# A gated cross-attention block with routed experts: normalisation of context and tokens moved from VectorE to ScalarE, and the gating slot reordered

## The reference

```python
x = x + tanh(g_xattn) * xattn(layernorm(x), ctx)   # 16 heads of 8, keys and values from the context
x = x + tanh(g_ffn) * ffn(layernorm(x))            # 8 experts, the best 2 of each token
```

## Time and profile before

| | |
|---|---|
| median of 3 runs | 401.38 us (397.15 to 403.08) |
| the profiled execution | 394.16 us, span 392.3 us |
| TensorE busy | 335.7 us (86% of the span) |
| VectorE busy | 236.9 us (60%) |
| ScalarE busy | 178.9 us (46%) |
| GpSimd busy | 105.5 us (27%) |

### The profile page before, as it was taken

How to read it: one execution, slowest core, us unless ns; L and a number is a source line. 1 busy time by engine, 2 the same in 40 slices (tenths; PEclk the granted TensorE clock), 3 DMA queues, 4 the chain that set the end, 5 groups by cost and what they waited for, 6 DMA issues and landing times.

```text
span 392.3 us, 8185 instructions
## 1 busy us (share of the span) xinstructions
PE 335.7 (86%) x2799; PEld 253.9 (65%) x2799; DVE 236.9 (60%) x935; ACT 178.9 (46%) x408; POOL 105.5 (27%) x188
## 2 busy tenths in 40 slices
PE   0869898789999789976999689979997998989693
PEld 0435565566787577855687477857785786677573
DVE  4693857665677456865477456866666566314553
ACT  1333445543745245543555246545654455334352
POOL 6473251434031603161031603150312001200000
PEclk9996989956999669976999869979998899558998
DMA  4411310363355431926055531815191500340000
GB/s 99 141 24 54 90 44 2 70 92 139 124 92 71 149 135 41 121 70 217 4 93 68 162 123 40 124 30 219 37 123 32 217 3 4 92 154 2 1 28 27
DMA packets 18456, 32.95 MB, mean 84 GB/s; under 512 B 4905, under 2 KB 11530, under 8 KB 18416
## 3 DMA queue, kind: packets, MB, share of 16 engines
q1 hardware_dynamic: 14270, 24.45, 24.9%
q0 software_dynamic: 3296, 7.93, 8.5%
q10 hardware_dynamic: 850, 0.05, 0.1%
HBM read 21.04 MB, written 2.21 MB: 59 GB/s over the span
## 4 chain that ended last, share of the span: by engine, by line
PE 36%; DVE 8%; DMA 6%; issue 3%; ACT 2%; POOL 1%; DVEq 0%; POOLq 0%
PE y L585 10%; PE c L532 5%; DMA gb<-gates_scratch 4%; PE s L510 3%; PE h L576 3%; PE ab L488 2%; PE h L577 2%; PE h L578 2%; DMA gates_scratch<-gatesT 2%; PE ab L549 2%; PE ab L556 1%; PE c L543 1%; PE ab L438 1%; DVE y_out L1073 1%; DVE negm L939 1%
## 5 line engine op out<-in xcount | busy, mean ns | idle before, releaser
L939 DVE TENSOR_REDUCE negm<-ab 128x4 f32<-128x308 f32 x128 | 59.5, 476 | 56.0 <-PE ab L488 55.0
L775 ACT ACTIVATE p<-s 77x512 f32<-77x512 f32 x128 | 74.9, 586 | 24.8 <-PE s L510 23.9
L510 PEld LDWEIGHTS s<-qs,ks 104*77 104x77 f32 x512 | 60.8, 168 | 11.0 <-issue 4.9
L585 PE MATMUL y<-w2s,hs 128*128 128x128 f32 x448 | 65.2, 292 | 1.3 <-ACT hs L782 1.3
L510 PE MATMUL s<-qs,ks 104*77 104x128 f32 x512 | 64.3, 254 | 0.1
L585 PEld LDWEIGHTS y<-w2s,hs 128*128 128x128 f32 x448 | 59.8, 207 | 1.8 <-ACT hs L782 1.7
L488 PE MATMUL ab<-ks,qs 96*128 96x312 f32 x128 | 55.0, 431 | 5.0 <-DVE negm L939 2.4
L532 PE MATMUL c<-p,vs 77*32 77x128 f32 x1024 | 54.5, 307 | 0.1
L782 ACT ACTIVATE hs<-u 128x512 f32<-128x512 f32 x56 | 35.1, 628 | 37.1 <-DVE u L1060 35.7
L1227 POOL TENSOR_SCALAR rs<-mv 128x1 f32<-128x1 f32 x32 | 8.0, 250 | 157.8 <-DVE mv L980 157.7
L1060 DVE SCALAR_TENSOR_TENSOR u<-h,gb 128x512 f32<-128x512 f32 x56 | 38.0, 681 | 17.9 <-DMA gb<-gates_scratch 16.0
(11 more groups left out here) (130 smaller groups left out, 525.8 us busy)
## 6 DMA issues: line engine op xcount, KB each, us to landing
gb<-gates_scratch SPq DMA_DIRECT2D x14, 768.0 KB, 5.7
gb<-gates_scratch SPq DMA_DIRECT2D x7, 512.0 KB, 3.8
qs<-q_hi SPq DMA_DIRECT2D x12, 256.0 KB, 5.5
ks<-k_hi SPq DMA_DIRECT2D x60, 39.0 KB
x_res<-in_x_dram POOLq DMA_DIRECT2D x8, 256.0 KB, 7.1
out_dram<-y_out POOLq DMA_DIRECT2D x8, 256.0 KB, 2.8
x_sb<-in_x_dram POOLq DMA_DIRECT2D x6, 256.0 KB, 3.7
qs<-q_lo SPq DMA_DIRECT2D x6, 256.0 KB, 7.7
```

Source lines behind the costliest of these rows:

```text
L510: mm = nc.tensor.matmul(p[0:N, T * i:T * i + T], ks[:, par, c, i, NP * j:NP * j + N], qs[:, par, c, T * j:T * j + T], start=True, stop=True)
L585: mm = nc.tensor.matmul(bank_y[:, D * b:D * b + D], hs[:, e % 2, T * b:T * b + T], w2s[:, e, :], start=(e == 0 and b == 0), stop=(e == E - ...
L775: nc.scalar.activation(p32[:, c, :], src, ACT.Exp).then_inc(p_done, 1)
L939: nc.vector.tensor_reduce(negm[:, :, c], bank_ab[bank][:, 0:J * NP].rearrange("t (i n) -> t i n", n=NP)[:, :, 0:N], AX.X, ALU.max, negate= ...
```

## The change

From tile 2 on, ScalarE computes context and tokens as scale * x + shift, with the root as scale and a shift = -mean * root, which GpSimd makes with two more instructions per chain (a negation of the mean and a product), so its chain has four instructions instead of two. Tiles 0 and 1 stay on VectorE; the eight instructions of each of tiles 2 to 7 leave it. On ScalarE the context stands behind exponent 1 of slot 2, the tokens behind exponent 2. In slot 1 VectorE starts the gates only behind `x_lo`, and takes its last two portions behind `mv`; the addition of `finish` moves behind the third portion. ScalarE does the first exponent of the next batch and the copy of the gates ahead of `evacuate_turned` in slot 1; in the other slots that order stays. TensorE and SyncE run the same instructions in the same order.

```diff
--- before.py
+++ after.py
@@ -51,7 +51,7 @@
 
 STATS = ["ctx_stats", "x_stats", "ctx_moments", "x_moments"]
 NORM = ["ctx_normed", "x_normed"]
-NORM_P = ["cvar_eps", "crstd", "var_eps", "rstd"]
+NORM_P = ["cvar_eps", "cneg", "crstd", "cshift", "var_eps", "neg", "rstd", "shift"]
 MAXP = ["hi", "lo"]
 POST = ["recip", "scaled", "x1", "stats", "moments", "normed"]
 LATE = ["top", "x_lo"]
@@ -133,7 +133,7 @@
         c_st = sb("c_st", [N, G, 6])
         x_mv = sb("x_mv", [T, G, 2])
         c_mv = sb("c_mv", [N, G, 2])
-        nrm = sb("nrm", [T, 4, G])
+        nrm = sb("nrm", [T, 6, G])
         xn = sb("xn", [T, G, D])
         cn = sb("cn", [N, G, L])
         xnT = sb("xnT", [D, GT])
@@ -729,6 +729,15 @@
                 nc.scalar.activation(q_hi[:, :], bank_ab[bank][:, :], ACT.Identity,
                                      bias=col(BQS)).then_inc(hi_q, 1)
 
+            def normalise(s, par, which):
+
+                n, dst, src, k, name = {"ctx": (N, cn, ctx_sb, 1, "cshift"), "x": (T, xn, x_sb, 4, "shift")}[which]
+                act.wait_ge(norm_p, at(NORM_P, s, name))
+                for b in range(G):
+                    ins = nc.scalar.activation(dst[:, b, :], src[:, par, b, :], ACT.Identity,
+                                               bias=nrm[0:n, k + 1, b:b + 1], scale=nrm[0:n, k, b:b + 1])
+                ins.then_inc(norm_d, 1)
+
             def split_query_rows(s, par):
 
                 if s == 0:
@@ -818,6 +827,8 @@
                         evacuate_heads(*near[-1])
                     if near[0]:
                         exponent(*near[0], 1)
+                    if j == 2 and third and i >= 0:
+                        normalise(*third, "ctx")
                     if j == 1 and exists(i - 1):
                         gate_exp(i - 1)
                     if j == 3 and third:
@@ -830,6 +841,8 @@
                         max_store(*near[2])
                     if near[0]:
                         exponent(*near[0], 2)
+                    if j == 2 and third and i >= 0:
+                        normalise(*third, "x")
                     if e[1] is not None:
                         squared(sf, e[1])
                     if j == 3 and third:
@@ -842,12 +855,14 @@
                         squared(sf, e[2])
                     if j == 2 and third:
                         evacuate_xT(third[0])
-                    if near[-1]:
-                        evacuate_turned(*near[-1])
-                    if near[1]:
+                    if j == 1 and near[1]:
                         exponent(*near[1], 0)
                     if j == 1 and spread(i - 1):
                         gate_rows(i - 1)
+                    if near[-1]:
+                        evacuate_turned(*near[-1])
+                    if j != 1 and near[1]:
+                        exponent(*near[1], 0)
 
             steps(step)
 
@@ -895,7 +910,7 @@
                 dve.wait_ge(norm_p, at(NORM_P, s, "rstd"))
                 for b in range(G):
                     ins = nc.vector.tensor_scalar(xn[:, b, :], x_sb[:, par, b, :], x_mv[:, b, 0:1],
-                                                  nrm[:, 3, b:b + 1], ALU.subtract, ALU.mult)
+                                                  nrm[:, 4, b:b + 1], ALU.subtract, ALU.mult)
                     if b == G - 1:
                         ins.then_inc(norm_d, 1)
                     if b % 2:
@@ -1139,7 +1154,7 @@
                     prepare = none
                     if j == 0 and third and i >= 0:
                         prepare = stats(*third)
-                    if j == 2 and third and i >= -1:
+                    if j == 2 and i == -1:
                         prepare = chained(normalise_ctx(*third), normalise_x(*third))
                     if j == 3 and third:
                         prepare = chained(low_keys(*third), (low_queries if i >= 0 else low_query_rows)(*third))
@@ -1160,26 +1175,21 @@
                         weighed(sf, pf, pending)
                     if near[-2]:
                         routed(*near[-2])
-                    take(gating)
                     take(top_scores)
                     take(post)
-                    take(gating)
                     take(top_scores)
-                    take(gating)
                     take(post)
-                    take(gating)
                     take(top_scores)
                     if near[-2]:
                         low_x(*near[-2])
                     take(gating)
                     take(gating)
-                    take(gating)
-                    if j == 1 and exists(i - 2) and not last(i - 2):
-                        finish(sf, pf)
                     take(top_scores)
                     if e[0] is not None:
                         gated_or_weighed(sf, pf, e[0])
                     take(gating)
+                    if j == 1 and exists(i - 2) and not last(i - 2):
+                        finish(sf, pf)
                     take(post)
                     take(top_scores)
                     take(post)
@@ -1213,12 +1223,16 @@
 
                 pool.wait_ge(stats_d, at(STATS, s, f"{which}_moments"))
                 apart(pool)
-                n, mv, k, scale, eps, names = {"ctx": (N, c_mv, 0, 1.0, EPS, ("cvar_eps", "crstd")),
-                                               "x": (T, x_mv, 2, 1.0 + EPS, EPS * EPS, ("var_eps", "rstd"))}[which]
+                n, mv, k, scale, eps, names = {"ctx": (N, c_mv, 0, 1.0, EPS, ("cneg", "crstd", "cshift")),
+                                               "x": (T, x_mv, 3, 1.0 + EPS, EPS * EPS, ("neg", "rstd", "shift"))}[which]
                 nc.gpsimd.tensor_scalar(nrm[0:n, k, :], mv[:, :, 1], scale, eps, ALU.mult, ALU.add).then_inc(norm_p, 1)
+                nc.gpsimd.tensor_scalar(nrm[0:n, k + 2, :], mv[:, :, 0], -1.0, None, ALU.mult).then_inc(norm_p, 1)
                 pool.wait_ge(norm_p, at(NORM_P, s, names[0]))
                 nc.gpsimd.tensor_tensor(nrm[0:n, k + 1, :], nrm[0:n, k, :], neg_half[0:n, :],
                                         ALU.pow).then_inc(norm_p, 1)
+                pool.wait_ge(norm_p, at(NORM_P, s, names[1]))
+                nc.gpsimd.tensor_tensor(nrm[0:n, k + 2, :], nrm[0:n, k + 2, :], nrm[0:n, k + 1, :],
+                                        ALU.mult).then_inc(norm_p, 1)
 
             def rstd(s, par, j):
                 n = G * s + j
```

## The result

The changed kernel has its median at 379.72 us over 4 runs (376.93 to 387.6); beside it the kernel before has 399.26 us (396.55 to 403.08). Intervals are computed from fast runs alone, those whose time is at most 1.5% above their kernel's fastest, while medians and ranges in the text are over all runs.

The account below looks back on a forecast made before the run. TensorE bounds the kernel, through its waits for VectorE's `cn` and the low clock behind them. Steps 2 to 4 give 13.8 us, the earlier L549 2.4, step 7 2: 18.2 us off 401.38, 383 us, range 368 to 396.

Parts of the forecast that it names:

- The copy of the gates: ScalarE, slot 1: copy ahead of the evacuation, store issues 2.4 us earlier in step 4, broadcast lands near 223.0.
- L414 waits for nothing, L585 waits 0.7 to 1 us, 8.1 us behind L549: TensorE, step 4: context transposes free, first output waits some 0.7 to 1 us for its square instead of 3.06.
- Steps 2, 3 and 4 give 13.8 us: These steps come down to step 5's length, 4.2 + 5.2 + 4.4 = 13.8 us, 6 of it clock.
- ScalarE's and GpSimd's prices: Normalising costs 1.5 us per four activations; GpSimd's negation 0.19 us and product 0.2 us.
- 0.4 us from the earlier L549 in steps 2 to 7: 2.4 us: VectorE's new gating order gives the moments earlier, moving the `xn2` transpose 0.4 us forward per step, 2.4 us together.
- rival 2: The low-clock stretch behind the L549 wait goes too, giving back 15 us: 368 us; chance 0.13.
- Step 7 2 us: Step 7's outputs lose a 1.1 us wait for a square behind the broadcast; 2 us with the clock.
- Step 0 has no gates to wait for: 0: Step 0, the first step, was counted as neither gaining nor losing.
- Normalising on ScalarE: Tiles 2 to 7: moving eight activations per tile off VectorE frees the context's transposes from the broadcast's landing.
- Rival 3: The waits go but the clock gives nothing back: gain 11 us, 390 us; chance 0.07.
- Rival 1: The stall moves on: gates' transfers land no earlier, L585 only 1.3 us earlier in five steps, 395 us; chance 0.19.
- Rival 4: Slower: negation and product at 1.04 us each make ScalarE late in every step, 412 us; chance 0.04.

Follow-up runs that it names:

- changed_again: The changed kernel with no edit, run once more in one set with orders_again: median 376.87 us.
- changed_third: The changed kernel with no edit, run again in the set of changed_fill: median 377.62 us.
- before_fill: The kernel before plus 6, 12 and 12 unused matmuls ahead of L414 in steps 2, 3 and 4: 394.85 us, against 405.19 for before.
- norm_act_order: The changed kernel with VectorE's gating order of before: median 391.34 us (383.41 to 397.27).
- orders_again: orders_only with no edit, run again in one set with changed_again: median 374.27 us.
- norm_only: The changed kernel with both engines' gating orders of before, so only the move to ScalarE: 403.99 us, against 405.05 for the kernel before.
- norm_dve_order: The changed kernel with ScalarE's gating-slot order of before: median 391.62 us (388.29 to 393.07).
- changed_fill: The changed kernel plus three unused matmuls ahead of L549 in steps 2 to 5: 384.27 us, 6.6 above changed_third.
- orders_only: Against the changed kernel, both new orders kept but normalising left on VectorE with GpSimd's chains of two: median 371.35 us (369.31 to 384.09).

## Why the prediction was right, point by point

- **The copy of the gates: right.** Forecast 2.4 us earlier; counted from L562 it came 2.8 us earlier in step 4 (0.32 instead of 3.09). The broadcast's end shows in `u`, 7.6 us behind L562 instead of 10.1, the very distance that was forecast (223.0 - 215.37). That the sum fits so well is luck: the store took 1.4 us instead of the 2.9 kept for it, the broadcast 5.6 instead of 3.8.
- **L414 waits for nothing, L585 waits 0.7 to 1 us, 8.1 us behind L549: right.** No wait, 0.93 us, 8.0 us. Of the signs named beforehand, "`u` waits under 1 us" holds in steps 2, 3, 5 and 6 and not in steps 1, 4 and 7 (1.2, 1.5 and 1.5 us), "eight activations under 3 us" is just missed, and of the signs of being wrong one came in small: L510 waits for exponents, 1.2 us in five waits.
- **Steps 2, 3 and 4 give 13.8 us: right.** 13.65 us in the profiled pair, and the same steps are as short in changed_again and changed_third. Of it 6 us were put on the clock. The stretches behind the first output, where the clock is what changed, gave 4.5 us of the 13.65; with the added matmuls of before_fill they gave 5.3.
- **ScalarE's and GpSimd's prices: right.** Four activations 1.54 and 1.65 us (forecast 1.5), the product 0.20 us (forecast 0.2, bounds 0.19 and 1.04). The price of one activation can also be had from a page. The Trainium skill, "ScalarE: Activation LUTs", section "What ACT_TABLE_LOAD costs", gives 186 ns plus 0.833 ns per column plus about 93 ns for each pointer operand; an estimate from these figures is 452 and 479 ns for 96 and 128 columns. The rows agree: 455 and 479.
- **VectorE's order, "0.4 us from the earlier L549 in steps 2 to 7: 2.4 us": the shift right, the worth too small.** L549 did move 0.4 us forward in step 4 (13.33 us behind slot 0's transposed maxima instead of 13.74). But undoing this order (norm_act_order) costs some 4 us even by its lowest run, and 12 to 14 by the medians. The forecast left out TensorE's wait at L495, 7.4 us in the kernel before and 1.5 in the changed one; with this order undone it is 5.9. How the larger cost comes about is not shown. A shorter low stretch behind L549, which would be rival 2 in part, is not the answer that the first pair gives: there it is as long as before. So rival 2 did not come.
- **"Step 7 2 us": too little.** The end behind step 7's L562 is 7.8 us shorter; its window from 345 to 355, at 0.50 before, has 1.00. In step 7 itself the first output comes 1.8 us earlier behind L562; the other 6.0 us go with a low stretch that lasts from about 334 to 356 in the kernel before and from 331 to 339 in the changed one. What keeps the clock low there is open: norm_act_order, whose copy is early, has a long stretch too, from about 338 to 359.
- **"Step 0 has no gates to wait for: 0", and the longer chains of tile 0, not priced at all: wrong.** These cost 3.6 us between changed_again and orders_again. I had listed ScalarE's new queue only against what the gates need. The evacuation of `cnT` stands in the same queue, behind all eight activations, and in step 0 TensorE waits for it.
- **Normalising on ScalarE as a part of the gain: wrong.** The forecast let L414's freedom from the landing come from the move. The orders alone give it nearly whole, since an earlier broadcast lets VectorE pass too (in steps 1 to 5 of orders_again L414 waits at most 0.6 us); norm_only shows no gain from the move without them.
- **Rival 3, no gain from the clock: refuted** by the 4.5 us above, and by 1.7 to 1.9 us per step in before_fill. The rule of the Trainium skill by which it would have been the forecast ("TensorE: Matmul & The Clock Gate", section "What's actually happening", under 1% of the span) does not hold for this kernel, whose clock falls again in the middle of the run: the mean is 0.870 before and 0.875 after, and the 4.5 us of three stretches alone are 1.1% of the span. **Rival 1**'s moved stall is what norm_only and norm_dve_order show; the changed kernel escaped it because the copy went early. **Rival 4** fell with the product at 0.20 us.

The gain was 19.5 us by the medians and 14.0 us between the profiled executions, where 18.2 was forecast; of the 3 us below the forecast total, 2 come from the kernel before, whose median was 399.26 in this comparison and 401.38 in the shown runs. Within the profiled pair the errors have both signs: the steps outside 2 to 4 and the end gave 5.3 us more than their 4.4, the start took 9.4 back. So a good total was partly luck.

## What to carry to other kernels

Where a long transfer's first link stands behind an unrelated wait in an engine's queue, put the link forward first: two orders made the whole gain here, and the move between engines none. Undo each part of a change by itself, since the part with the most code may be the one without a gain. Work moved to another engine stands in that queue in every step, also in those whose waits you did not study, so go down its queue instruction by instruction and price the start-up, where nothing hides a longer chain. Filling TensorE's idle time keeps its clock up, but brings nothing as long as the next thing it needs comes no earlier.

## What the runs showed of the hardware

- The low clock is not tied to idle time in the stretch itself: in the changed kernel's profile it was 0.50 from 52 to 79 us, with TensorE's rows busy for 26.78 of them.
- A wait of 1.5 us at L488 was followed by 0.50 (changed_again, 68 to 72 us); 0.23 us at the same place by 1.00. But a longer wait need not be: in step 2 of norm_dve_order L585 waits 2.34 us until 145.68, and the clock stays full behind it. The same holds in its step 3 (1.98 us), and for 1.51 us in step 3 of changed_fill. So the length of one wait does not tell whether the clock falls.

```profile
146.00:156.00 10.00, 10.00 (x90) 7.48 (x89) 5.35 (x18) 6.95 (x16) 0.80 (x2) 1.00 0.25 102
```

- One kernel scatters widely with nothing changed: before took 393.8 to 416.4 us in 28 runs of three sets, and orders_only 369.3 to 384.1. Differences of 2 or 3 us between kernels need one set and many rounds.
- In step 4 the store of the gates was faster when started early, and the broadcast slower: the broadcast issues 1.4 us behind the store (216.59 to 217.98) instead of 2.9. The kernel before also has 1.4 us in steps 5 and 6, where GpSimd has no tile left to load. That loads beside it make this difference fits, but was not tried. Its landing then took longer, up to 5.6 us (217.98 to `u` at 223.60) instead of 3.8, so 0.3 us of the copy's 2.8 was lost on the way.
